# GNN layer end on one Trainium2 core: Wo and W2 products from high and low parts, W1 chunk by chunk

## The chip, the cores and the metric

The kernel runs on one core of one Trainium2 chip. The metric is the device time of one execution in microseconds (us); of several runs the median counts.

## The reference, cut to what matters

Four graph network layers follow each other on 1250 nodes with 512 features, everything in float32. The second of them is a stack of two attention layers over 40000 edges; the change is in the end of each of these two:

```python
for l in range(L):                       # L = 2, H = 8, D = 512, F = 256
    q = ((x @ Wq[l].T + bq[l]) * scaling).reshape(n, H, DH)
    k = (x @ Wk[l].T).reshape(n, H, DH)
    v = (x @ Wv[l].T).reshape(n, H, DH)
    ...                                  # softmax over the edges of each target
    agg = jax.ops.segment_sum(w[:, :, None] * v[srcidx], tgt, num_segments=n)
    attn = agg.reshape(n, D) @ Wo[l].T + bo[l]
    x = _batchnorm(x + attn, g1[l], beta1[l])
    ff = jax.nn.relu(x @ W1[l].T + b1[l]) @ W2[l].T + b2[l]
    x = _batchnorm(x + ff, g2[l], beta2[l])
return _layernorm(x, ln_g, ln_b)
```

The batch norm is over the nodes, so each feature needs all 1250 nodes of its row before it can be normalised. The other three layers, which take most of the 2642 us, are not touched.

## The kernel before

Features lie on partitions. `k.x1t` holds x as 4 blocks (KC) of 128 features by NP = 1280 node columns; `at.agg` holds the attention's result in the same form. The columns go in three pieces of C3 = 417 (WIDE). For each of the two layers `layer1` calls `attend`, whose block ends with a barrier of all engines, and then `finish_layer`. Each engine has its own program there, written out by hand; semaphores join them, and each engine's instructions run in the order in which the code has them.

TensorE in `finish_layer`: `turn(0, KC)` transposes Wo (four sets of four 128x128 transposes, into banks 0 and 1 in turn), and ScalarE copies each set to `wo` (L1581). `product(wo, at.agg, ...)` makes 12 outputs (4 feature blocks, three pieces each), each a sum over 4 input chunks, in a ring of four banks (2 to 5), as whole float32 matmuls (L1556). After 4 of them come the transposes of W1 and W2 (OTHERS). The product with W1 makes 6 outputs of 4 chunks, the hidden layer `hid`, by ScalarE's Relu (L1598); its first output waits chunk by chunk for the normalised x (`x_ready`), and after two outputs (WEIGHTS) the 16 transposes of the next layer's Wq come in between. The product with W2 makes 12 outputs of 2 chunks. Then, in layer 0 alone, `project_tensor` begins with the next layer's q, k and v. These already work with high and low parts: a high part is the value rounded to the type float32r (`F32R`), the low part is the rest, and three matmuls (high x high, high x low, low x high) stand for one float32 product (L1142).

VectorE in `add_and_norm`: for each output it adds bias and x from the bank (L1643, which frees the bank); after three outputs it takes the statistics of that feature block (L102, L104, L108), ScalarE takes the root (L1585), and one block later VectorE makes scale and shift (L1624 to L1626) and normalises (L1631). In the second norm of layer 0 ScalarE writes the high part and the whole x (L1608, L1611) and VectorE the low part (L1636). Between the two norms it makes the low parts of the next Wq (L1133; ScalarE's high parts: L1126).

GpSimd, in layer 1 alone, adds a row to ten blocks (L1530) once all of x is normalised the first time. SyncE loads W1, W2 and Wq at the block's start, Wk after the last output of Wo, and Wv when Wq's transposes are done.

## Time and profile before

| | us |
|---|---|
| median of three runs | 2642.36 (2640.85 to 2644.28) |
| the profiled execution | 2644.61 |
| its span, first to last instruction | 2642.9 |
| TensorE matmuls busy | 2421.8 (92%) |
| VectorE busy | 2058.8 (78%) |
| ScalarE busy | 1713.2 (65%) |
| GpSimd busy | 1090.7 (41%) |

The span is cut by the page into 40 slices of 66 us; a digit is the busy share in tenths. Layer 0's end runs from 1111 us and layer 1's from 1591 us of the span, and both are small parts of it, so they are read from the trace, by timeline. There a row is a start, a duration, the engine, the line of the kernel, the operation with output and inputs, how often it comes in a row, and in brackets how long the engine had been idle and what released it. A whole float32 matmul stands in the trace as two records, and the records of matmuls overlap a little: the pace is the distance between starts, not the duration of one. A stretch of windows gives for each engine the busy time and the number of instructions, then TensorE's granted clock as a share of 2.4 GHz.

### The profile page before, as it was taken

The numbers are of one execution on the slowest core, as the hardware profiler recorded it, in microseconds if no ns is written. First come the engines' busy times: TensorE is split into PE (matmuls) and PEld (weight loads), VectorE is DVE, ScalarE is ACT, GpSimd is POOL, SyncE is SP. The second block draws the span as 40 slices with busy tenths as digits, with TensorE's granted clock in tenths as the row PEclk, the third lists the DMA queues.
The fourth block names the chain that finished last, engine by engine and source line by source line (L and its number), as shares of the span: only waits on it lengthen the run. The fifth ranks groups of instructions, "written<-read, shape, count | busy, mean of one in ns | idle before, by whom it ended". The sixth has DMA issues, their size and how long they took to land. (4 is left out here: it accounts for less than half of the span.)

```text
span 2642.9 us, 44424 instructions
## 1 busy us (share of the span) xinstructions
PE 2421.8 (92%) x12731; PEld 1923.7 (73%) x12731; DVE 2058.8 (78%) x4101; ACT 1713.2 (65%) x3755; POOL 1090.7 (41%) x1061
## 2 busy tenths in 40 slices
PE   6999699998998999999999998798999999986887
PEld 3777455556798999858799994366777777765776
DVE  8789799998636888645588983756999999865757
ACT  1889788885726777614477871233999999835560
POOL 1776655524203454000254421115777777700311
PEclk9999899999999999999999999898999999988999
DMA  2004122213254434103444521124777777812101
GB/s 93 3 3 125 32 69 66 65 36 100 88 185 108 117 101 109 53 32 135 112 121 117 110 45 64 48 76 142 244 238 238 238 237 238 203 53 68 48 9 40
DMA packets 116594, 278.11 MB, mean 105 GB/s; under 512 B 24039, under 2 KB 38314, under 8 KB 116462
## 3 DMA queue, kind: packets, MB, share of 16 engines
q0 software_dynamic: 51328, 138.78, 19.3%
q1 hardware_dynamic: 65134, 137.65, 16.7%
q8 instruction: 73, 1.20, 0.2%
q14 instruction: 59, 0.48, 0.1%
HBM read 208.80 MB, written 59.43 MB: 101 GB/s over the span
## 5 line engine op out<-in xcount | busy, mean ns | idle before, releaser
L806 POOL DMA_INDIRECT feature_rows<-in_edge_attr,id_idx x352 | 341.9, 971 | 448.6 <-POOLq L1507 226.6
L2081 POOL DMA_INDIRECT x_got<-table_dram,src_idx x352 | 376.0, 1068 | 110.0 <-issue 82.0
L1441 DVE TENSOR_TENSOR pt_low<-bank,pt_high 128x640 fp32r<-128x640 f32 x320 | 262.8, 822 | 53.8 <-ACT pt_high L1404 52.6
L761 ACT ACTIVATE hot_rest<-hot_dst,slot_w 128x128 bf16<-128x128 bf16 x864 | 272.9, 399 | 43.9 <-DVE hot_dst L711 43.5
L1404 ACT CAST pt_high<-bank 128x640 fp32r<-128x640 f32 x320 | 220.3, 689 | 113.5 <-PE bank L1355 113.5
L2225 DVE TENSOR_TENSOR msg<-bank,x_got 128x512 f32<-128x512 f32 x352 | 236.6, 683 | 43.8 <-DMA x_got<-table_dram,src_idx 19.3
L1435 DVE CUSTOM_DVE_ANT_0 p<-bank,log_counts 128x1254 f32<-128x1254 f32 x160 | 232.8, 1455 | 14.1 <-PE bank L1338 14.1
L1355 PE MATMUL bank<-ident,p 128*128 128x128 f32 x1600 | 229.3, 275 | 2.4 <-DVE pt_low L1441 2.4
L1396 ACT ACTIVATE p<-p,bound 128x1254 f32<-128x1254 f32 x160 | 215.5, 1347 | 9.3 <-DVE bound L1435 9.3
L1366 PE MATMUL bank<-pt_high,val 128*128 128x256 f32 x800 | 212.7, 300 | 0.9 <-DVE agg_t L1447 0.9
L2205 DVE SCALAR_TENSOR_TENSOR msg_low<-msg,msg_high 128x512 fp32r<-128x512 f32 x308 | 209.3, 680 | 0.0
L2170 ACT ACTIVATE msg_high<-msg 128x512 fp32r<-128x512 f32 x308 | 193.5, 628 | 18.5 <-DVE msg L2225 17.8
L1367 PE MATMUL bank<-pt_low,val 128*128 128x256 f32 x800 | 199.7, 284 | 0.0
L1355 PEld LDWEIGHTS bank<-ident,p 128*128 128x128 f32 x1600 | 190.7, 142 | 11.4 <-issue 3.2
L217 POOL DMA_INDIRECT slots_dram<-rec,pos x152 | 152.2, 1002 | 112.9 <-issue 95.1
L1337 PE MATMUL bank<-keys,queries 128*128 128x418 f32 x480 | 186.2, 388 | 12.8 <-DVE bound L1435 7.5
L1338 PE MATMUL bank<-keys,queries_low 128*128 128x418 f32 x480 | 172.2, 359 | 0.0
L782 PE MATMUL bank<-hot_src,hot_rest 128*128 128x417 bf16 x864 | 170.8, 339 | 0.0
L809 POOL DMA_DIRECT2D features_dram<-feature_rows x88 | 51.2, 582 | 274.6 <-DMA feature_rows<-in_edge_attr,id_idx 274.6
L582 PE MATMUL bank<-row_hot,col_part 125*128 125x352 f32 x840 | 156.6, 339 | 8.6 <-ACT col_part L625 4.5
L582 PEld LDWEIGHTS bank<-row_hot,col_part 125*128 125x128 f32 x840 | 135.4, 190 | 29.5 <-issue 18.6
L1367 PEld LDWEIGHTS bank<-pt_low,val 128*128 128x128 f32 x800 | 154.2, 193 | 0.0
(435 smaller groups left out, 6347.4 us busy)
## 6 DMA issues: line engine op xcount, KB each, us to landing
features_dram<-feature_rows POOLq DMA_DIRECT2D x88, 256.0 KB
edge_got<-features_dram SPq DMA_DIRECT2D x88, 256.0 KB, 3.6
qk_dram<-qk_high SPq DMA_DIRECT2D x16, 640.0 KB, 2.9
qk_dram<-qk_low SPq DMA_DIRECT2D x16, 640.0 KB, 4.2
keys<-qk_dram SPq DMA_DIRECT2D x32, 320.0 KB, 4.9
queries<-qk_dram SPq DMA_DIRECT2D x32, 320.0 KB, 6.9
queries_low<-qk_dram SPq DMA_DIRECT2D x32, 320.0 KB, 8.8
acc_a<-zeros SPq DMA_DIRECT2D x1, 6400.0 KB
```

The lines of the kernel that those rows point to most:

```text
L582: m = pe.matmul(ps_p[:, q, :], col_part[0:EP, u, q, :], row_hot[0:EP, u, :], start=(c == 0), stop=(c == PE_COLS - 1))
L761: last = act.activation(hot_rest[:, u, j, q, :], hot_dst[:, u, :, j], ACT.Copy, scale=k.slot_w[:, 1 + q, bass.ds(tile0 + j, 1)])
L806: pool.indirect_dma_start(out=self.rows[:, u, t % GT * ED:(t % GT + 1) * ED], out_offset=None, in_=self.a.edge_attr_128, in_offset=bass.In ...
L1355: t = pe.transpose(unit(i)[:, j * P:(j + 1) * P], p[:, n % AHEAD, (u * HALF + j) * P:(u * HALF + j + 1) * P], k.ident[:])
L1366: pe.matmul(to, v, p_high[:, slot, j, :], start=(u == 0 and j == 0), stop=False)
L1367: x = pe.matmul(to, v, p_low[:, slot, j, :], start=False, stop=(u == 1 and j == HALF - 1))
L1396: act.activation(rows, rows, ACT.Exp, bias=bound[:, n % 4:n % 4 + 1], scale=-1.0, accum_out=sums[:, n // (2 * NB) % 2, n % NB, n // NB % 2 ...
L1404: act.copy(p_high[:, made % 3, :, n % 2 * P:(n % 2 + 1) * P], unit(2 * n + u).rearrange("p (j n) -> p j n", n=P)).then_inc(high_made, 1)
L1435: dve.tensor_tensor_reduce(out=thirds(p[:, n % AHEAD, :]), in0=k.bank[:, 0:3, 0:THIRD], in1=thirds(k.log_counts[:, n % NB, :]), scale=-1.0 ...
L1441: dve.tensor_tensor(p_low[:, made % 3, :, columns], unit(2 * n + u).rearrange("p (j n) -> p j n", n=P), p_high[:, made % 3, :, columns].bi ...
L2081: pool.indirect_dma_start(out=xg[:, g % XRING, j, :], out_offset=None, in_=k.table_dram, in_offset=bass.IndirectOffsetOnAxis(ap=k.src_idx[ ...
L2225: dve.tensor_tensor(msg[:, j, :], k.bank[:, 2 + j, :], xg[:, r, j, :], ALU.add).then_inc(added_x, 1)
```

## The change

The function `finish_layer` is changed, and nothing else.

- Wo and the aggregate are split. ScalarE writes the aggregate's high part chunk by chunk (four casts of 128x1280), each ahead of the copy of a turned chunk of Wo, which is now that chunk's high part. VectorE makes the low part of each. They lie where the next layer's high and low x come later.
- The third and fourth set of Wo's transposes wait for the low part of the first and second (`w_lowered`).
- The first six outputs of Wo are made together, in a ring of six banks: for each input chunk three passes for each of six outputs. Then W1 and W2 are transposed, then come the other six outputs one by one.
- All ten copies of turned weights now stand ahead of ScalarE's first root. W2's two low parts are made by VectorE after the seventh add.
- W1 stays whole float32 but goes chunk by chunk over all six outputs. Two sets of the next Wq's transposes stand ahead of the last chunk, two behind W1.
- ScalarE makes the hidden layer twice, rounded and whole; VectorE makes its low part (L1717 in the changed file) before W2's adds. W2 takes three passes.
- The pieces are 418, 418 and 416 columns (EVEN) in place of 417.

```diff
+    FP = FF // P
+    agg_parts = [Region(nc, at.wq_at - 4 * KC * NP * (2 - q), at.wq_at - 4 * KC * NP * (1 - q)).take(f"agg_{n}", [P, KC, NP], F32R) for q, n in enumerate(("high", "low"))]
+    r = Region(nc, at.wo_rows_end, at.wq_at - 2 * 4 * KC * NP)
+    wo = r.take("wo_in", [P, 2, KC, D], F32R)
     w1 = r.take("w1_in", [P, KC, FF], F32)
-    w2 = r.take("w2_in", [P, FF // P, D], F32)
...
-    hid = r.take("hidden", [P, FF // P, NP], F32)
-    FP = FF // P
-
-    OTHERS = 4
-    WEIGHTS = 2
+    hid_whole = r.take("hidden_whole", [P, 2, C3 + 1], F32)
+
+    w2 = Region(nc, at.wo_rows_end - 4 * KC * D - 2048, at.wo_rows_end).take("w2_in", [P, 2, FP, D], F32R)
+
+    over_agg = Region(nc, at.agg_end - 4 * KC * NP, at.agg_end)
+    hid = over_agg.take("hidden", [P, 2, FP, NP], F32R)
+    RING = 6
+    EARLY = 2
+
     affine_ready = S("bn_affine_ready")
 
-    turns = [(0, c, KC, wo[:, c, :]) for c in range(KC)] + [(1, c, FP, w1[:, c, :]) for c in range(KC)] + [(2, c, KC, w2[:, c, :]) for c in range(FP)]
+    turns = [(0, c, KC, wo[:, 0, c, :]) for c in range(KC)] + [(1, c, FP, w1[:, c, :]) for c in range(KC)] + [(2, c, KC, w2[:, 0, c, :]) for c in range(FP)]
+    low_parts = [(n, wo[:, 1, n, :]) for n in range(KC)] + [(2 * KC + c, w2[:, 1, c, :]) for c in range(FP)]
...
@@ -1535,36 +1542,65 @@
                 for n, (j, c, o, to) in list(enumerate(turns))[first:end]:
                     if c == 0:
                         pe.wait_ge(w_loaded[j], 16)
-                    if n >= 2:
+                    if 2 <= n < 2 + KC:
+                        pe.wait_ge(w_lowered, n - 1)
+                    elif n >= 2:
                         pe.wait_ge(w_copied, n - 1)
                     turned(pe, k, n % 2, rows[j], c, o).then_inc(w_turned, 1)
 
...
+            def out_of(n, ring):
+                o, (c, wide) = n // 3, EVEN[n % 3]
+                return k.bank[:, 2 + n % ring, 0:wide], slice(o * P, (o + 1) * P), slice(c, c + wide)
+
+            def rows_of_wo(n, i):
+                to, o, c = out_of(n, RING)
+                for q, s in ((0, 0), (0, 1), (1, 0)):
+                    m = pe.matmul(to, wo[:, q, i, o], agg_parts[s][:, i, c], start=(i == 0 and q + s == 0), stop=(i == KC - 1 and q == 1))
+                return m
 
             turn(0, KC)
-            pe.wait_ge(w_copied, KC)
-            product(wo, at.agg, KC, KC, o_done, o_added, None, lambda: turn(KC, len(turns)), OTHERS)
+            for i in range(KC):
+                pe.wait_ge(w_lowered, i + 1)
+                pe.wait_ge(agg_low_made, i + 1)
+                for n in range(RING):
+                    m = rows_of_wo(n, i)
+                    if i == KC - 1:
+                        m.then_inc(o_done, 1)
+            turn(KC, len(turns))
+            for n in range(RING, 3 * KC):
+                pe.wait_ge(o_added, n - RING + 1)
+                for i in range(KC):
+                    m = rows_of_wo(n, i)
+                m.then_inc(o_done, 1)
             pe.wait_ge(w_copied, len(turns))
-            pe.wait_ge(o_added, 9)
-            product(w1, k.x1t, KC, FP, h_done, h_copied, x_ready, turn_following if following else None, WEIGHTS)
-            pe.wait_ge(h_copied, 3 * FP)
-            product(w2, hid, FP, KC, f_done, f_added)
+            for i in range(KC):
+                if i == KC - 1 and following:
+                    turn_following(0, EARLY)
+                pe.wait_ge(x_ready, i + 1)
+                for n in range(3 * FP):
+                    to, o, c = out_of(n, RING)
+                    if i == 0:
+                        pe.wait_ge(o_added, 3 * KC - RING + n + 1)
+                    m = pe.matmul(to, w1[:, i, o], k.x1t[:, i, c], start=(i == 0), stop=(i == KC - 1))
+                    if i == KC - 1:
+                        m.then_inc(h_done, 1)
+            if following:
+                turn_following(EARLY, KC)
+            pe.wait_ge(w_lowered, len(low_parts))
+            for n in range(3 * KC):
+                if n < 3:
+                    pe.wait_ge(h_low_made, 3 * (FP - 1) + n + 1)
+                if n >= 4:
+                    pe.wait_ge(f_added, n - 3)
+                to, o, c = out_of(n, 4)
+                for i in range(FP):
+                    for q, s in ((0, 0), (0, 1), (1, 0)):
+                        m = pe.matmul(to, w2[:, q, i, o], hid[:, s, i, c], start=(i == 0 and q + s == 0), stop=(i == FP - 1 and q == 1))
+                m.then_inc(f_done, 1)
 
...
@@ -1577,6 +1613,8 @@
         def _(act):
             def copies(first, end):
                 for n, (j, c, o, to) in list(enumerate(turns))[first:end]:
+                    if n < KC:
+                        act.copy(agg_parts[0][:, n, :], at.agg[:, n, :]).then_inc(agg_high_made, 1)
                     act.wait_ge(w_turned, n + 1)
                     act.copy(to, k.bank[:, n % 2, 0:o * P]).then_inc(w_copied, 1)
 
@@ -1584,19 +1622,22 @@
                 act.wait_ge(var_ready, turn * KC + o + 1)
                 act.sqrt(norm.dev[:, o:o + 1], norm.var[:, o:o + 1]).then_inc(dev_ready, 1)
 
-            copies(0, KC)
+            copies(0, len(turns))
             for o in range(KC):
                 root(0, o)
-                if o == 0:
-                    copies(KC, len(turns))
+            if following:
+                for c in range(EARLY):
+                    weight_high(act, k, following, 0, c)
             for n in range(3 * FP):
-                if following and n == WEIGHTS:
-                    for j in range(KC):
-                        weight_high(act, k, following, 0, j)
                 act.wait_ge(h_done, n + 1)
-                c = WIDE[n % 3]
-                act.activation(hid[:, n // 3, c:c + C3], k.bank[:, 2 + n % 4, 0:C3], ACT.Relu,
-                               bias=at.vec[:, at.B1 + n // 3:at.B1 + n // 3 + 1]).then_inc(h_copied, 1)
+                (c, wide), bias = EVEN[n % 3], at.vec[:, at.B1 + n // 3:at.B1 + n // 3 + 1]
+                act.activation(hid[:, 0, n // 3, c:c + wide], k.bank[:, 2 + n % RING, 0:wide], ACT.Relu, bias=bias)
+                if n >= 2:
+                    act.wait_ge(h_low_made, n - 1)
+                act.activation(hid_whole[:, n % 2, 0:wide], k.bank[:, 2 + n % RING, 0:wide], ACT.Relu, bias=bias).then_inc(h_copied, 1)
+            if following:
+                for c in range(EARLY, KC):
+                    weight_high(act, k, following, 0, c)
             if following:
                 act.copy(following.x_high[:, :, W3:NP], k.x1t[:, :, W3:NP])
             for o in range(KC):
@@ -1616,7 +1657,11 @@
         def _(dve):
             me = Steps(nc, dve, at.sem("finish_dve"))
 
-            def add_and_norm(done, added, bias, gain, beta, turn):
+            def low_part(n, to):
+                dve.wait_ge(w_copied, n + 1)
+                dve.tensor_tensor(to, k.bank[:, n % 2, :], turns[n][3].bitcast(F32), ALU.subtract).then_inc(w_lowered, 1)
+
+            def add_and_norm(done, added, bias, gain, beta, turn, ring):
 
                 def normalise(o):
                     dve.wait_ge(dev_ready, turn * KC + o + 1)
@@ -1637,15 +1682,19 @@
...
                 for n in range(3 * KC):
-                    o, c = n // 3, WIDE[n % 3]
-                    x = k.x1t[:, o, c:c + C3]
+                    o, (c, wide) = n // 3, EVEN[n % 3]
+                    end = min(c + wide, W3)
+                    x = k.x1t[:, o, c:end]
                     dve.wait_ge(done, n + 1)
-                    dve.scalar_tensor_tensor(x, k.bank[:, 2 + n % 4, 0:C3], at.vec[:, bias + o:bias + o + 1], x, ALU.add, ALU.add).then_inc(added, 1)
+                    dve.scalar_tensor_tensor(x, k.bank[:, 2 + n % ring, 0:end - c], at.vec[:, bias + o:bias + o + 1], x, ALU.add, ALU.add).then_inc(added, 1)
                     if n % 3 == 0 and o:
                         normalise(o - 1)
+                    if not turn and n == RING:
+                        for m, to in low_parts[KC:]:
+                            low_part(m, to)
                     if n % 3 == 2:
                         dve.wait_ge(added, n + 1)
-                        norm.stats(dve, me, o, *(k.x1t[:, o, c:min(c + C3, N)] for c in WIDE))
+                        norm.stats(dve, me, o, *(k.x1t[:, o, c:min(c + wide, N)] for c, wide in EVEN))
                         norm.variance(dve, me, var_ready, o, o + 1)
                         if turn and following and o:
                             lower(o - 1)
@@ -1653,12 +1702,23 @@
                 if turn and following:
                     lower(KC - 1)
 
-            add_and_norm(o_done, o_added, at.BO, at.G1, at.BETA1, 0)
+            for i in range(KC):
+                dve.wait_ge(agg_high_made, i + 1)
+                dve.tensor_tensor(agg_parts[1][:, i, :], at.agg[:, i, :], agg_parts[0][:, i, :].bitcast(F32), ALU.subtract).then_inc(agg_low_made, 1)
+                low_part(*low_parts[i])
+            add_and_norm(o_done, o_added, at.BO, at.G1, at.BETA1, 0, RING)
 
             if following:
-                for c in range(KC):
+                for c in range(EARLY):
                     weight_low(dve, k, following, 0, c)
-            add_and_norm(f_done, f_added, at.B2, at.G2, at.BETA2, 1)
+            for n in range(3 * FP):
+                c, wide = EVEN[n % 3]
+                dve.wait_ge(h_copied, n + 1)
+                dve.tensor_tensor(hid[:, 1, n // 3, c:c + wide], hid_whole[:, n % 2, 0:wide], hid[:, 0, n // 3, c:c + wide].bitcast(F32), ALU.subtract).then_inc(h_low_made, 1)
+            if following:
+                for c in range(EARLY, KC):
+                    weight_low(dve, k, following, 0, c)
+            add_and_norm(f_done, f_added, at.B2, at.G2, at.BETA2, 1, 4)
             if following:
                 project_vector(dve, me, k, following)
             else:
```

ScalarE's program at the start of layer 0's end. Before:

```order
L1581 COPY wo_in<-bank 128x512 x4
L1585 ACT_TABLE_LOAD
L1585 ACTIVATE bn_dev<-bn_var 128x1
L1581 COPY w_in<-bank 128x256 x4
L1581 COPY w_in<-bank 128x512 x2
```

And now, the same place (`bn_dev<-bn_var` is the root):

```order
L1617 CAST agg_high<-agg_t 128x1280
L1619 CAST wo_in<-bank 128x512
...
L1619 COPY w_in<-bank 128x256 x4
L1619 CAST w_in<-bank 128x512 x2
L1623 ACT_TABLE_LOAD
L1623 ACTIVATE bn_dev<-bn_var 128x1 x4
```

Casts of the aggregate have come in front of the copies (four pairs in all), and the table load has moved behind the copies of W1 and W2.

TensorE from the end of the Wo product in layer 0 to the start of W2. Before:

```order
L1556 MATMUL bank<-agg_t,wo_in 128x417 x32
L1556 MATMUL bank<-x1t,w_in 128x417 x8
L1055 MATMUL bank<-ident,wqkv_rows_a_7127 128x128 x16
L1556 MATMUL bank<-x1t,w_in 128x417 x16
L1556 MATMUL bank<-hidden,w_in 128x417 x24
```

And now, the end of the third round over W1's six outputs, and the fourth:

```order
L1588 MATMUL bank<-x1t,w_in 128x418 x2
L1588 MATMUL bank<-x1t,w_in 128x416
L1055 MATMUL bank<-ident,wqkv_rows_a_7127 128x128 x8
L1588 MATMUL bank<-x1t,w_in 128x418 x2
L1588 MATMUL bank<-x1t,w_in 128x416
L1588 MATMUL bank<-x1t,w_in 128x418 x2
L1588 MATMUL bank<-x1t,w_in 128x416
L1055 MATMUL bank<-ident,wqkv_rows_a_7127 128x128 x8
L1602 MATMUL bank<-hidden,w_in 128x418 x12
```

The transposes of Wq have been split, eight ahead of W1's last round and eight behind it.

VectorE from the end of the first norm to the second norm's first adds, in layer 0. Before:

```order
L1625 TENSOR_TENSOR bn_shift<-bn_mean_var,bn_scale 128x1
L1626 TENSOR_TENSOR bn_shift<-vec,bn_shift 128x1
L1631 TENSOR_SCALAR x1t<-x1t,bn_scale,bn_shift 128x1251
L1133 TENSOR_TENSOR wqkv_a_7132<-bank,wqkv_a_7132 128x512 x4
L1643 SCALAR_TENSOR_TENSOR x1t<-bank,vec,x1t 128x417 x3
```

And now:

```order
L1670 TENSOR_TENSOR bn_shift<-bn_mean_var,bn_scale 128x1
L1671 TENSOR_TENSOR bn_shift<-vec,bn_shift 128x1
L1676 TENSOR_SCALAR x1t<-x1t,bn_scale,bn_shift 128x1251
L1133 TENSOR_TENSOR wqkv_a_7132<-bank,wqkv_a_7132 128x512 x2
L1717 TENSOR_TENSOR hidden<-hidden_whole,hidden 128x418 x2
L1717 TENSOR_TENSOR hidden<-hidden_whole,hidden 128x416
L1717 TENSOR_TENSOR hidden<-hidden_whole,hidden 128x418 x2
L1717 TENSOR_TENSOR hidden<-hidden_whole,hidden 128x416
L1133 TENSOR_TENSOR wqkv_a_7132<-bank,wqkv_a_7132 128x512 x2
L1689 SCALAR_TENSOR_TENSOR x1t<-bank,vec,x1t 128x418 x2
```

Six subtractions for the hidden layer have come between the low parts of Wq and the adds.

## Rows read from the trace of the kernel before

**Rows 1.** The page, TensorE's granted clock in 40 slices (9: 0.9 or more):
```profile
PEclk9999899999999999999999999898999999988999
```

**Rows 2.** Windows (PE, PEld, DVE, ACT, POOL busy, PEclk), layer 0: Wo part, second norm:
```profile
1115.50:1152.00 36.50, 35.94 (x113) 19.98 (x114) 17.51 (x41) 4.26 (x10) 0.00 (x0) 1.00 0.08 30
...
1181.00:1199.00 18.00, 16.75 (x57) 10.19 (x56) 17.31 (x44) 9.19 (x9) 0.00 (x0) 1.00 0.00 0
```

**Rows 3.** Timeline of TensorE, layer 0:
```profile
1111.13 3.73 PE L1055 MATMUL bank<-ident,wo_rows 128*128 128x128 f32 x16 [1.92 <-PEq L1308]
1115.54 11.47 PE L1556 MATMUL bank<-agg_t,wo_in 128*128 128x417 f32 x32 [0.68 <-ACT wo_in L1581]
...
1129.58 22.57 PE L1556 MATMUL bank<-agg_t,wo_in 128*128 128x417 f32 x64
1151.98 2.26 PE L1556 MATMUL bank<-x1t,w_in 128*128 128x417 f32 x6
1156.94 3.77 PE L1556 MATMUL bank<-x1t,w_in 128*128 128x417 f32 x10 [2.70 <-DVE x1t L1631]
...
1163.70 11.37 PE L1556 MATMUL bank<-x1t,w_in 128*128 128x417 f32 x32
1175.77 17.07 PE L1556 MATMUL bank<-hidden,w_in 128*128 128x417 f32 x48 [0.70 <-ACT hidden L1598]
```

**Rows 4.** The same, layer 1:
```profile
1590.96 3.73 PE L1055 MATMUL bank<-ident,wo_rows 128*128 128x128 f32 x16 [1.92 <-PEq L1308]
1595.37 6.97 PE L1556 MATMUL bank<-agg_t,wo_in 128*128 128x417 f32 x13 [0.68 <-ACT wo_in L1581]
...
1633.97 2.26 PE L1556 MATMUL bank<-x1t,w_in 128*128 128x417 f32 x6
1638.94 14.97 PE L1556 MATMUL bank<-x1t,w_in 128*128 128x417 f32 x42 [2.71 <-DVE x1t L1631]
```

**Rows 5.** Timeline, the next layer's q: first and last of 13 low-part passes:
```profile
1196.73 0.35 PE L1142 MATMUL bank<-px_low,wqkv_a 128*128 128x418 f32 x1
...
1203.62 0.35 PE L1142 MATMUL bank<-px_low,wqkv_a 128*128 128x418 f32 x1
```

**Rows 6.** Groups of ScalarE: busy us, mean ns of one, idle before:
```profile
L1928 ACT CAST at<-at_raw 128x1280 fp32r<-128x1280 f32 x10 | 12.6, 1266 | 39.5 <-PE bank L1048 39.5
...
L1208 ACT COPY qk_whole<-bank 128x418 f32<-128x418 f32 x16 | 8.1, 509 | 28.0 <-PE bank L1142 28.0
...
L1598 ACT ACTIVATE hidden<-bank,vec 128x417 f32<-128x417 f32 x12 | 7.3, 610 | 27.5 <-PE bank L1556 27.5
...
L1581 ACT COPY wo_in<-bank 128x512 f32<-128x512 f32 x8 | 4.7, 586 | 14.7 <-PE bank L1055 14.7
```

**Rows 7.** Groups of VectorE, the same columns:
```profile
L1133 DVE TENSOR_TENSOR wqkv_a<-bank,wqkv_a 128x512 fp32r<-128x512 f32 x16 | 10.6, 686 | 12.5 <-ACT wqkv_a L1126 12.5
...
L1636 DVE TENSOR_TENSOR px_low<-x1t,px_high 128x1280 fp32r<-128x1280 f32 x3 | 4.4, 1482 | 0.0
...
L1636 DVE TENSOR_TENSOR px_low<-x1t,px_high 128x418 fp32r<-128x418 f32 x2 | 1.2, 595 | 2.4 <-ACT x1t L1611 2.4
```

**Rows 8.** Timeline of VectorE, second norm: layer 0, and layer 1's first statistics:
```profile
1180.96 1.58 DVE L102 BATCH_NORM_STATS2 bn_pieces<-x1t 128x6 f32<-128x417 f32 x3
...
1205.44 0.62 DVE L1636 TENSOR_TENSOR px_low<-x1t,px_high 128x444 fp32r<-128x444 f32 x1 [0.80 <-ACT x1t L1611]
...
1659.80 1.58 DVE L102 BATCH_NORM_STATS2 bn_pieces<-x1t 128x6 f32<-128x417 f32 x3
```

**Rows 9.** Windows (columns as in rows 2): start of layer 0's and layer 1's end:
```profile
1111.00:1115.50 4.50, 3.73 (x16) 3.00 (x16) 0.00 (x0) 2.35 (x4) 0.00 (x0) 0.55 0.73 233
...
1595.30:1599.80 4.50, 4.43 (x7) 2.28 (x8) 0.00 (x0) 1.30 (x2) 0.00 (x0) 0.51 0.83 304
```

**Rows 10.** Windows (columns as in rows 2), two other places, TensorE partly busy:
```profile
612.00:622.00 10.00, 6.63 (x51) 5.37 (x50) 7.22 (x2) 7.02 (x12) 3.66 (x4) 1.00 1.15 347
625.00:632.00 7.00, 3.41 (x13) 2.25 (x11) 6.93 (x3) 5.93 (x6) 7.00 (x3) 0.88 0.49 148
```

More of the change, by code:

```diff
@@ L1537, in turn, with turn_following @@
                         pe.wait_ge(w_loaded[j], 16)
-                    if n >= 2:
+                    if 2 <= n < 2 + KC:
+                        pe.wait_ge(w_lowered, n - 1)
+                    elif n >= 2:
                         pe.wait_ge(w_copied, n - 1)
                     turned(pe, k, n % 2, rows[j], c, o).then_inc(w_turned, 1)
-            def turn_following():
-                for c in range(KC):
+            def turn_following(first, end):
+                for c in range(first, end):
@@ L1544, in turn_following @@
                     turn_weight(pe, k, following, 0, c)
-            def product(w, x, inputs, outputs, done, free, arrive=None, others=None, at_n=None):
-                for n in range(3 * outputs):
-                    o, c = n // 3, WIDE[n % 3]
-                    if others and n == at_n:
-                        others()
-                    if n >= 4:
-                        pe.wait_ge(free, n - 3)
-                    for i in range(inputs):
-                        if arrive and n == 0:
-                            pe.wait_ge(arrive, i + 1)
-                        m = pe.matmul(k.bank[:, 2 + n % 4, 0:C3], w[:, i, o * P:(o + 1) * P], x[:, i, c:c + C3],
-                                      start=(i == 0), stop=(i == inputs - 1))
-                    m.then_inc(done, 1)
@@ L1654, in add_and_norm @@
                     lower(KC - 1)
-            add_and_norm(o_done, o_added, at.BO, at.G1, at.BETA1, 0)
+            for i in range(KC):
[3 more added lines that the diff above has]
+            add_and_norm(o_done, o_added, at.BO, at.G1, at.BETA1, 0, RING)
             if following:
-                for c in range(KC):
+                for c in range(EARLY):
                     weight_low(dve, k, following, 0, c)
-            add_and_norm(f_done, f_added, at.B2, at.G2, at.BETA2, 1)
+            for n in range(3 * FP):
[6 more added lines that the diff above has]
+            add_and_norm(f_done, f_added, at.B2, at.G2, at.BETA2, 1, 4)
             if following:
```

4 lines of the change are left out of this document (1 added, 3 removed).

## The prediction, on record before the changed kernel ran

> **What bounds the kernel now.** I read the page's forty slices first [rows 1]: the changed function is entered twice, for layer 0 near 1111 us and for layer 1 near 1591 us, some 90 us each, and TensorE's clock is near full there. Then the timeline of TensorE in each of the two [rows 3, 4]. The reader should see three parts. The Wo product runs without a gap, 96 records 0.35 us apart; a whole float32 product of 417 columns is two records, so 0.70 us. Then TensorE does three outputs' first chunks of W1 and waits 2.70 us for the normalised x. Then W1 and W2 run again at 0.70 us a product. Up to the end of W1 TensorE ends last: over the Wo part VectorE is busy 17.51 of 36.50 us [rows 2]. From there VectorE ends last: 17.31 of 18.00 us busy in the second norm [rows 2], which is 5.8 us for each of its blocks of 128 features, where TensorE needs 3 x 1.40 = 4.2. That chain begins with the statistics at 1180.96 and ends with the last low piece at 1206.06 [rows 8]. So what counts is how much earlier the second norm's VectorE chain may begin, in layer 0 and in layer 1 (1659.80 now). Cheaper W2 products are worth nothing behind that point.
>
> **The change, part by part.** All in span time of layer 0, then what differs in layer 1.
>
> (a) *The start, +2.2 us in each layer.* Four input chunks of Wo must now be split into high and low, and the aggregate too. ScalarE makes a high part of 128x1280 in 1.27 us [rows 6], then copies the turned weight in 0.59; VectorE follows with 1.48 for the aggregate's low part and 0.69 for the weight's [rows 7]. From 1111.1: high part 1112.4, low part 1113.9, weight low part 1114.6. The third set of transposes waits for that, the fourth for the second one, which is there 1.48 + 0.69 us later, at 1116.8. All four sets stand ahead of the first product in TensorE's queue. A set takes a quarter of 3.73 us [rows 3], so the first product starts at 1117.75, against 1115.54 now. Queued behind this wait is only the product; VectorE and ScalarE are ahead of it from then on, since a chunk takes TensorE 3.4 us and VectorE 2.2. The price can't be much below (VectorE's 4.3 us of work is in series); it could be 3.5 with slow handovers.
>
> (b) *The Wo product, -6.1 us in each.* 48 products become 144 passes. The projection's passes of the same 418 columns and type stand in the trace: 13 records of the low part from 1196.73 to 1203.62, 12 steps of three passes [rows 5], so 0.574 for three and 0.191 for one. 48 x 0.70 = 33.6 becomes 48 x 0.574 = 27.5. The transposes of W1 and W2 stay between (2.7 us), now after six outputs in place of four. The Trainium skill, page "TensorE: Matmul & The Clock Gate", section "Back-to-back issue gap", gives N/2.4 + 2.5 ns for a warm matmul, 0.177 us at 418 columns; the rows show 0.191, and they decide. By the page the product would take 25.4 us, the layers would gain 2 us more each, and the time would be about 2625 us.
>
> (c) *The clock, +2.2 us in layer 0, 0 in layer 1.* TensorE is at 1.2 GHz (granted clock 0.50 to 0.55) through the transposes in both layers, after some microseconds with little work [rows 9]. In layer 0 it was at full clock from the first product, in layer 1 only 4.4 us after it: 13 records took 6.97 us [rows 4]. The change spreads the transposes out and so gives TensorE less to do ahead of the first product. I take layer 1's case for both: 4.4 us at half clock lose 2.2, which layer 1 has already. Bounds: 0 in both (2.2 better in layer 1, 2.2 better in layer 0), or much longer, which is a rival below.
>
> (d) *W1, chunk by chunk.* Its 24 products stay whole float32, 16.8 us. What goes is the wait of 2.70 for the last norm [rows 3]: the last chunk is needed only 12.6 us after the product's start. VectorE has to be done by then. Its first add comes late (when six outputs are almost complete, about 1130.7), and ScalarE's table load of 1.28 us now stands behind ten copies, so the first root comes at about 1137.8 and VectorE stands for 2.5 us. From there it needs about 5.8 us a block, plus 1.4 for W2's two low parts, against 6.9 of TensorE for three outputs: its last normalised block comes near 1157.6, and TensorE asks for it near 1163. So the wait is gone, with 5 us of cover. W1's first round waits for the banks of the last adds; at most 0.5. In layer 0 eight of the next layer's transposes stay inside W1 (1.0 us), the other eight go behind it, where TensorE would wait for the hidden parts.
>
> W1 now starts at 1151.98 and ends at 1175.07 [rows 3]. After: start at 1151.98 + 2.2 - 6.1 + 2.2 = 1150.3, end at + 16.8 + 1.0 = 1168.1, **7.0 earlier**. Layer 1: 1633.97 + 2.2 - 6.1 = 1630.1, end at 1646.9, against 1638.94 + 14.97 = 1653.91 [rows 4]: **7.0 earlier**.
>
> (e) *The hidden's low parts, +0.9 in layer 0, about 0 in layer 1.* The six outputs of W1 are now completed 0.70 apart in the last round, the first 3.5 us before W1's end. For each ScalarE does two activations; alone one takes 0.61, in a row 0.51 [rows 6]. I take 1.1 for a pair, 6.6 in all, so 3.1 past W1's end; with VectorE's subtraction of 0.60 [rows 7] 3.8. W2's first output needs the fourth low part, 1.6 past the end, and is done at +2.8; the third, needing the sixth, at +5.0; its add ends at +5.8. Today the statistics behind the third add begin at 1180.96, 5.9 after W1's end [rows 8]. In layer 0 two high and two low parts of the next Wq stand ahead of the adds on VectorE (at most 2 x 0.69, partly waiting for ScalarE): adds from +4.9, the third done at +6.8, so 0.9 later. With ScalarE at 1.22 a pair it is 0.7 more in each. In layer 1 GpSimd's ten additions, which wait for the last normalised x, now partly run beside VectorE's subtractions; no row shows this pair together, I take 0 and keep 0.5 for the range.
>
> (f) *W2, 0.* 72 passes, 1.15 us an output, three in 3.4, while VectorE needs 5.8 a block. All of it lies beside VectorE. The loads of K's and V's weights move by -2 and +5 us, and are used tens of microseconds later.
>
> **Sum.** Layer 0: 7.0 - 0.9 = 6.1. Layer 1: 7.0. Together 13.1 us. The profiled execution took 2644.61 us (span 2642.90) and would take 2631.5; the median of the three runs, 2642.36, is 2.25 us below that execution, so the forecast is **2629.3 us**. What comes behind each layer's end waits for its barrier and moves as a whole: GpSimd's gathers beside the attention don't end last.
>
> **Rivals.**
> *The clock doesn't fall back on us, or less* (first products at 2.4 GHz in both layers, as in layer 0 now): 4.4 us more, 17.5 in all, 2624.9. For it: layer 0 now. Against: fewer transposes in a row before the product.
> *The clock falls in W2.* TensorE would be busy 3.4 of 5.8 us there, 59%. At 66% the clock stayed 1.00, at 49% it came to 0.88 [rows 10]; 59% is between. At 1.2 GHz an output takes 2.3 us and three 6.9, more than VectorE's 5.8, so TensorE would be the bound, by 1.1 us a block in layer 0 and 1.5 in layer 1, until its full load brings the clock back. Some 4 us in all: gain 9, 2633.3.
> *The splitting chains are slower than their rows.* 1.5 us more at each start and 2.5 more at each hidden chain, from handovers that the prices above don't hold: 8 us, gain 5, 2637.3, within 0.2%.
> *The clock stays at half through the first six outputs, and the kernel is slower.* Their 72 passes take 13.75 us at full clock and 27.5 at half, so 11.6 more than I count in each layer: 23.2 - 13.1 = 10.1 us slower, 2652.5. It decides once half clock lasts over 17 us of products in each layer (4.4 counted, plus twice 6.55). Against it: 4.4 us in layer 1 [rows 4, 9], and TensorE has no gap after the first product.
> That three passes are no cheaper than a whole product is excluded by rows 5.
>
> **How the numbers follow.** Forecast 0.58; clock better 0.12; clock falling in W2 0.17; slower chains 0.09; clock stuck 0.04. The 8 in 10 range takes in the first three with their bounds (a: 1.3 us a layer, e: 0.7 a layer): 2624.0 to 2636.0. A difference under 0.2%, 5.3 us, is about what can't be told from none. Faster by more: 0.88; within: 0.08; slower: 0.04.
>
> **What would show it.** Right: the first product 6 to 7 us after the first transpose; passes 0.19 us apart; no wait of TensorE for the norm inside W1; W1's end about 57 us after the first transpose in layer 0 and 56 in layer 1 (63.9 and 62.95 now); VectorE busy over 90% from the third add to the layer's end, and the statistics of the second norm near 1175 and 1653 less what layer 0 gained. Wrong: TensorE waiting for x in W1, a granted clock below 1 after the first 5 us of products or in W2, or more than 6 us from W1's end to the second norm's first statistics in layer 1.

## The result, and the profile after

Four runs of the changed kernel have a median of 2630.02 us (2627.87 to 2632.13), four of the kernel before 2643.32 (2640.85 to 2648.54). The ratio is 0.9947, with a 95% interval from 0.9931 to 0.9963: 13.3 us shorter, faster by more than 0.2%. The forecast was 2629.3 within 2624.0 to 2636.0. The profiled execution's span is 2630.4 us, 12.5 less than before.

The whole moved as forecast, but not in the way that it was forecast. To compare the two layers' ends I measure from the first of Wo's transposes in each. From there to the first statistics of the second norm, behind which VectorE is the bound, it took 69.83 us in layer 0 and 68.84 in layer 1 [rows 3, 4, 8]. Now it takes 62.74 and 65.42: 7.1 and 3.4 us less, where 6.1 and 7.0 were forecast.

TensorE in layer 0, timeline (start, duration, engine, line, operation, count, idle time before and its releaser), against [rows 3]:

```profile
1112.82 1.94 PE L1055 MATMUL bank<-ident,wo_rows 128*128 128x128 f32 x8 [1.92 <-PEq L1308]
1116.23 1.11 PE L1055 MATMUL bank<-ident,wo_rows 128*128 128x128 f32 x4 [1.47 <-DVE wo_in L1662]
1118.23 1.12 PE L1055 MATMUL bank<-ident,wo_rows 128*128 128x128 f32 x4 [0.88 <-DVE wo_in L1662]
1119.00 0.70 PE L1562 MATMUL bank<-agg_high,wo_in 128*128 128x418 f32 x1
...
1151.21 13.10 PE L1588 MATMUL bank<-x1t,w_in 128*128 128x418 f32 x36
1164.14 1.04 PE L1055 MATMUL bank<-ident,wqkv_rows_a 128*128 128x128 f32 x8
1165.02 4.37 PE L1588 MATMUL bank<-x1t,w_in 128*128 128x418 f32 x12
1169.23 1.04 PE L1055 MATMUL bank<-ident,wqkv_rows_a 128*128 128x128 f32 x8
1170.80 11.59 PE L1602 MATMUL bank<-hidden,w_in 128*128 128x418 f32 x60 [0.53 <-DVE hidden L1717]
```

The two waits of the later transposes for VectorE's low parts are there, 1.47 and 0.88 us. The first product comes 6.18 us after the first transpose. W1 starts at 38.4 us and runs without a wait to 56.6; the 2.70 us before the last norm's chunk are gone.

Layer 1, the same engine, its first transposes and from W1 on, against [rows 4]:

```profile
1584.95 1.94 PE L1055 MATMUL bank<-ident,wo_rows 128*128 128x128 f32 x8 [1.92 <-PEq L1308]
...
1622.84 17.31 PE L1588 MATMUL bank<-x1t,w_in 128*128 128x418 f32 x48
1643.29 14.44 PE L1602 MATMUL bank<-hidden,w_in 128*128 128x418 f32 x60 [3.14 <-DVE hidden L1717]
```

W1 ends at 55.2 us, as in layer 0, but then TensorE stands for 3.14 us for the hidden layer's low parts. What VectorE and GpSimd do in that time, timeline:

```profile
1629.48 0.93 DVE L1676 TENSOR_SCALAR x1t<-x1t,bn_scale,bn_shift 128x1251 f32<-128x1251 f32 x1
1637.82 0.59 DVE L1717 TENSOR_TENSOR hidden<-hidden_whole,hidden 128x418 fp32r<-128x418 f32 x1 [7.41 <-ACT hidden_whole L1637]
1638.82 6.40 DVE L1717 TENSOR_TENSOR hidden<-hidden_whole,hidden 128x418 fp32r<-128x418 f32 x5 [0.40 <-ACT hidden_whole L1637]
1645.75 0.65 DVE L1689 SCALAR_TENSOR_TENSOR x1t<-bank,vec,x1t 128x418 f32<-128x418 f32 x1 [0.53 <-PE bank L1602]
1647.84 0.65 DVE L1689 SCALAR_TENSOR_TENSOR x1t<-bank,vec,x1t 128x418 f32<-128x418 f32 x1 [1.43 <-PE bank L1602]
...
1630.56 13.71 POOL L1537 TENSOR_TENSOR x_rows<-x_rows,ln_b_row 128x512 f32<-128x512 f32 x10 [76.92 <-DVE x1t L1676]
```

The last five subtractions take 6.40 us, back to back, where in layer 0 each took 0.59 at a pace of 1.00. All but the last of them lie beside GpSimd's ten additions, which end at 1644.27. Then the adds come 2.1 and 1.8 us apart. TensorE's granted clock tells why, in windows of the same stretch (PE, PEld, DVE, ACT, POOL busy with counts, clock, DMA):

```profile
1640.20:1643.30 3.10, 0.01 (x1) 0.04 (x1) 3.10 (x3) 2.31 (x6) 3.10 (x3) 0.86 0.00 0
1643.30:1650.40 7.10, 7.10 (x23) 6.82 (x24) 3.91 (x6) 0.48 (x1) 0.97 (x1) 0.58 0.00 0
```

In the gap the clock fell, and W2's first outputs ran at 1.2 GHz (0.58 over the stretch). So two of the signs that the prediction named as "wrong" are there: more than 6 us from W1's end to the statistics in layer 1 (10.2), and a granted clock below 1 in W2.

The rest of the 12.5 us: layer 0's end began 1.7 us later than before, the attention between was 0.6 shorter, and the stages behind layer 1 together 3.1 shorter. The code of these stages is the same, and the four runs of before lie 7.7 us apart; I count this as scatter. Its sum, 2.0 us, is what made the forecast of the whole look better than its parts.

### The profile page after: what moved, and what is told of

The parts are those of the page before. It is cut to its first block and busy times, and to the rows that moved or that the text cites. A ratio compares the mean times of both kernels' runs of the same rounds, so it can differ in the third digit from the quotient of the medians.

```text
span 2630.4 us, 44774 instructions
## 1 busy us (share of the span) xinstructions
PE 2405.5 (91%) x12875; PEld 1955.3 (74%) x12875; DVE 2088.5 (79%) x4133; ACT 1726.7 (66%) x3775; POOL 1093.5 (42%) x1061
```

## Experiments

All kernels below ran where the kernel before took 2838.5 to 2838.9 us in place of 2643 (2811.5 for four of them: the changed kernel's third execution, the two kernels under "The order alone, and Wo alone", and the second execution of W2 whole with spread transposes), and where whole times of one kernel scatter over 11 to 24 us. The layers' ends are hardly touched by that, so the experiments are read by their local times, each from one traced execution. The kernel before has a trace from the first setting only. Two more executions of the changed kernel show how far local times repeat.

> The changed kernel itself, beside the combinations on one chip. Both theories: first product 6.2 us after the first transpose, W1's end at 55 to 57 us in both layers. Theory A (GpSimd's additions slow VectorE's subtractions in layer 1): the five subtractions together take 6.4 us there again, and the second norm's first statistics come 7.9 us after W1's end if the clock stays, 10.2 if it falls; in layer 0 6.2. Rival B (it was one execution's accident): subtractions of 0.59 us in layer 1.

> The changed kernel once more, as the measure for the combination beside it. Both theories: its own local times again, statistics at 62.7 and 65.4 us; the whole 0.994 to 0.996 of the kernel before.

Statistics came at 62.84 and 65.53 in the first, at 61.83 and 62.90 in the second. W1 began between 37.5 and 38.5 us in layer 0 and between 37.7 and 38.0 in layer 1: after the first product the half clock lasted 4.3 us in layer 0 of the first trace and 2.6 in that of the third execution. The five subtractions took 6.40 and 6.41 us in layer 1. In the second the clock stayed up after the gap: 7.9 us from W1's end to the statistics in layer 1, not 10.2. So the slow subtractions come each time and cost 2.1 us (7.9 against 5.8 where nothing disturbs them, below); the clock's fall comes on top in some executions and costs 2.3. The ratios of the whole times to the kernel before were 0.996 (0.9938 to 0.9982) and 0.9945 (0.9926 to 0.9965).

**GpSimd out of the way.**

```diff
-            pool.wait_ge(x_ready, KC)
```

> GpSimd's ten additions no longer wait for the normalised x; all else as in the changed kernel. Theory A (VectorE's subtractions in layer 1 are slowed by GpSimd's additions beside them, and TensorE's clock falls in the gap that this makes): subtractions 0.59 us each, last one as in layer 0 within 2 us of W1's end, no gap of 3.1 us before W2, granted clock 1.00 in W2, statistics at about 60.5 us after layer 1's first transpose in place of 65.4; the additions now lie beside the first norm, which has some us of cover. Rival B (the gap is the clock's or the splitting chain's own doing): statistics stay at 65.

The six subtractions of layer 1 in this kernel (min/median/max ns), and then those of the changed kernel:

```profile
L1716 DVE TENSOR_TENSOR hidden<-hidden_whole,hidden x6: 591/594/595, 1757.5 to 1762.5; 128x418 fp32r<-128x418 f32 x4, 128x416 fp32r<-128x416 f32 x2
```

```profile
L1717 DVE TENSOR_TENSOR hidden<-hidden_whole,hidden x6: 574/1411/1660, 1637.8 to 1644.6; 128x418 fp32r<-128x418 f32 x4, 128x416 fp32r<-128x416 f32 x2
```

Only the time of GpSimd's work was changed, and the subtractions fell from a median of 1411 to 594 ns. W2 began 1.4 us after W1's end at a granted clock of 1.00, the statistics came 5.8 us after it, at 60.86 us in place of 65.42. The additions now ran beside the first norm's adds and statistics, and those kept their times:

```profile
1715.00 12.49 POOL L1536 TENSOR_TENSOR x_rows<-x_rows,ln_b_row 128x512 f32<-128x512 f32 x10 [68.39 <-DMA x_rows<-x_dram]
...
1723.51 1.80 DVE L1688 SCALAR_TENSOR_TENSOR x1t<-bank,vec,x1t 128x418 f32<-128x418 f32 x3 [9.37 <-PE bank L1561]
1725.34 1.58 DVE L102 BATCH_NORM_STATS2 bn_pieces<-x1t 128x6 f32<-128x418 f32 x3
```

So the cause of the slow subtractions is shown: VectorE's subtraction of two tiles in SBUF beside GpSimd's addition, not VectorE's work beside GpSimd as such. That the clock's fall comes from the gap which they make is only argued: behind a gap of 1.4 us it stayed up in two traces, behind one of 3.1 us it stayed up in two and fell in two. The Trainium skill says of the subtractions, on the page "SBUF — State Buffer", section "Who interferes with whom": a VectorE instruction with two SBUF inputs contends with a GpSimd instruction that reads SBUF, one with at most one SBUF input does not, outside the modes in which it uses two ports. The adds, with one input in a bank, and the statistics agree with it.

**W2 whole.**

```diff
-                    for q, s in ((0, 0), (0, 1), (1, 0)):
-                        m = pe.matmul(to, w2[:, q, i, o], hid[:, s, i, c], ...)
+                    m = pe.matmul(to, w2[:, i, o], hid[:, i, c], start=(i == 0), stop=(i == FP - 1))
...
-                if n >= 2:
-                    act.wait_ge(h_low_made, n - 1)
-                act.activation(hid_whole[:, n % 2, 0:wide], ...)
...
-                dve.tensor_tensor(hid[:, 1, n // 3, c:c + wide], hid_whole[:, n % 2, 0:wide], ...)
```

> W2 and the hidden layer go back to whole float32 (one activation an output, no subtraction, no low parts of W2); Wo's passes and W1's order stay as in the changed kernel. Theory A (W2's passes gain nothing behind VectorE, and their splitting costs): in layer 0 the second norm's first statistics stay within 1 us of 62.7 us after the first transpose; in layer 1, where the subtractions ran beside GpSimd, they come at 61 in place of 65.4, so the whole is some 4 us shorter than the changed kernel. Rival B (the passes carry part of the gain): statistics in both layers 2 us or more later than now, the whole longer.

Statistics at 61.92 and 60.22 us: 0.8 and 5.2 sooner than in the changed kernel's first execution, but 0.1 later and 2.7 sooner than in its third. Counted from W1's start the scatter of the start drops out: in layer 0 the statistics come 24.35 us after it in all three executions of the changed kernel and 23.67 here; in layer 1 23.10 with three passes and early additions, and 21.91 here. So W2's three passes gain nothing, and their splitting costs 0.7 us in layer 0 and 1.2 in layer 1, where GpSimd and the clock come on top. GpSimd's additions took 12.27 us here, as before the change (12.28), and 13.71 beside the subtractions.

**The start.**

```diff
-            turn(0, KC)
+            turn(0, 2)
             for i in range(KC):
...
+                if i + 2 < KC:
+                    turn(i + 2, i + 3)
```

> The third and fourth set of Wo's transposes go behind the first and second chunk of the product. Theory A (the start is paid by TensorE standing for the low parts of weights that it needs only later): first product 3.4 us after the first transpose in place of 6.2, W1's start and all behind it 2 to 2.5 us earlier in each layer. Rival B (the clock takes it back: more of the products fall in the half clock): W1's start less than 1 us earlier.

```profile
1695.69 1.94 PE L1055 MATMUL bank<-ident,wo_rows 128*128 128x128 f32 x8 [1.92 <-PEq L1308]
1699.10 0.72 PE L1562 MATMUL bank<-agg_high,wo_in 128*128 128x418 f32 x1 [1.47 <-DVE wo_in L1664]
```

The first product came at 3.41 us. W1 began at 36.5 us in both layers: 1.9 and 1.4 us sooner than in the changed kernel's first execution, 1.0 and 1.1 sooner than in its third. That is at or above the rival's 1 and below the 2 to 2.5 of theory A. Of the 2.8 us at the first product 0.7 are no gain: the two sets of transposes come later, between the chunks, 0.36 us each. The half clock lasted from the first product for 4.7 us here, against 4.3 and 3.5 in the changed kernel's first trace; at half the pace that takes back 0.2 and 0.6. This execution is also the second case in which the clock stayed up through the gap of layer 1:

```profile
1749.50:1752.60 3.10, 0.03 (x1) 0.00 (x0) 3.10 (x3) 2.31 (x6) 3.10 (x3) 1.00 0.00 0
1752.60:1757.40 4.80, 4.60 (x23) 4.24 (x24) 3.88 (x5) 0.57 (x1) 1.06 (x1) 1.00 0.00 0
```

The same gap, the same instructions, and a clock of 1.00 where it was 0.86 and 0.58: statistics 7.9 us after W1's end in layer 1.

**W1 output by output.**

```diff
-            for i in range(KC):
...
-                for n in range(3 * FP):
+            for n in range(3 * FP):
+                to, o, c = out_of(n, RING)
+                pe.wait_ge(o_added, 3 * KC - RING + n + 1)
+                for i in range(KC):
```

> W1 goes output by output again (the next Wq's first transposes in the wait of the first output), the rest as in the changed kernel. Theory A (chunk by chunk hides the wait for the last norm): a wait of 4 to 4.5 us inside W1's first output, W1's end 4 us later in both layers; statistics 3 us later in layer 0, but in layer 1 not later, since the hidden parts then come 2.8 us apart and mostly after GpSimd is done. Rival B: no wait, W1's end within 1 us.

```profile
1737.44 1.56 PE L1588 MATMUL bank<-x1t,w_in 128*128 128x418 f32 x4
1739.91 0.97 PE L1588 MATMUL bank<-x1t,w_in 128*128 128x418 f32 x2 [0.91 <-DVE x1t L1675]
1745.08 17.58 PE L1588 MATMUL bank<-x1t,w_in 128*128 128x418 f32 x42 [4.20 <-DVE x1t L1675]
```

In layer 1 the waits are 0.91 and 4.20 us (0.90 and 3.33 in layer 0). Behind them 42 records take 17.58 us, where they took 14.97 before [rows 4], so here too a part ran at half clock (granted 0.50 behind the wait). W1's end came 5.4 and 8.1 us later than in the changed kernel's first execution, not 4; the statistics 4.3 and 2.0 us later. I had expected layer 1 not to lose, and that was wrong by the clock's share and because the wait is longer with a Wo product that ends sooner.

**Wo whole, W2 as in the changed kernel.** Its high and low parts are left out; ring, chunks and the rest stay.

```diff
-                for q, s in ((0, 0), (0, 1), (1, 0)):
-                    m = pe.matmul(to, wo[:, q, i, o], agg_parts[s][:, i, c], ...)
+                return pe.matmul(to, wo[:, i, o], at.agg[:, i, c], start=(i == 0), stop=(i == KC - 1))
```

> Wo goes back to whole float32 products, in the same order (six outputs by chunk, then six one by one), with no high and low parts of the aggregate or of Wo; W1 and W2 as in the changed kernel. Forecast's terms: start at 4.4 us in place of 6.2, 48 products of 0.70 in place of 144 passes of 0.191, so W1's start 6.1 less 1.8 to 4.0 (with the clock) later than in the changed kernel, at 40.7 to 42.9 us, and W1's end at 58.6 to 60.8 in layer 0. If the passes' gain was eaten by their splitting and the clock, W1's start is no later than 38.4 us.

First product at 3.53 us (it no longer waits for all four sets), W1's start at 39.9 and 40.8, its end at 57.8 in both. Against the three executions of the changed kernel the three passes of Wo, with what they cost at the start, are worth 1.1 to 2.1 us in layer 0 and 2.5 to 2.8 in layer 1. The forecast had 1.7 and 3.9 by its own terms (6.1 less 2.2 for the start, and in layer 0 less 2.2 for the clock); the kernel with Wo whole starts 0.9 us sooner than the one before, which those terms didn't hold. Its statistics came at 63.97 and 65.80 us. In layer 1 the gap before W2 was only 2.15 us, since GpSimd's additions overlapped fewer subtractions, and the clock fell all the same:

```profile
1745.35:1747.50 2.15, 0.00 (x0) 0.03 (x1) 2.00 (x2) 1.75 (x5) 1.05 (x1) 0.99 0.00 0
1747.50:1751.00 3.50, 3.50 (x10) 3.35 (x11) 1.84 (x3) 0.99 (x2) 0.00 (x0) 0.52 0.00 0
```

**The order alone, and Wo alone.** Two kernels that combine these edits: the first with Wo, W2 and the hidden layer whole, the second with W2 whole and W1 output by output.

> Of the change only the order is kept (rings of six, Wo's first six outputs and W1 chunk by chunk, Wq's transposes split in two); Wo, W2 and the hidden layer are whole float32. Theory A (most of the gain is the order of W1, which hides the wait for the norm; the passes of Wo add little at this start, those of W2 nothing): W1's end at 57.8 us after the first transpose in both layers, first statistics of the second norm at 63.6 in layer 0 and 62.7 in layer 1, so 6 us a layer before the old kernel's 69.8 and 68.8, and better than the changed kernel in layer 1 (65.4). Rival B (the passes carry the gain): statistics at 67 or later.

> Of the change only Wo's three passes and its order are kept; W1 goes output by output, W2 and the hidden layer are whole float32. Theory A: the wait for the last norm comes back, 4 to 5 us long, and TensorE's clock may fall in it: W1's end at 61 to 63 us, statistics at 67 to 68 us in both layers, so 1 to 3 us a layer before the old kernel. Rival B (the passes carry the gain): statistics at 64 or sooner.

The order alone gave 64.65 and 62.66, Wo's passes with their order 67.79 and 66.28. The first is 5.2 and 6.2 us sooner than the kernel before, the second 2.0 and 2.6. Theory A's numbers hold within 1.1 us; the largest miss is W1's end with the order alone in layer 0, 58.9 for 57.8. The four stages tell where the gains lie (us; layer 0, layer 1):

| | first transpose to first product | to W1's start | W1 | W1's end to statistics |
|---|---|---|---|---|
| before | 4.41, 4.41 | 36.44, 38.60 | 23.09, 19.94 | 5.89, 5.89 |
| order alone | 3.53, 3.52 | 37.45, 37.22 | 17.87, 16.99 | 5.80, 4.93 |
| Wo's passes with their order | 6.19, 6.19 | 31.44, 32.13 | 24.37, 23.03 | 5.79, 4.93 |
| changed, first execution | 6.18, 6.18 | 32.21, 31.71 | 18.18, 17.30 | 6.17, 10.23 |

With the order alone the gain in W1 itself is 5.2 us in layer 0 and 3.0 in layer 1. In layer 0 the kernel before had a second wait inside W1, 1.03 us for Wq's low part, besides the one for the norm, and eight more transposes; layer 1 had only its wait of 2.71. The other 3.3 us of layer 1 are a start that waits chunk by chunk (0.9), a shorter stretch at half clock behind the first product (in the 1.4 us of the second stage), and a W2 that no longer waits for the whole hidden layer (1.0). In layer 0 the second stage is 1.0 longer, with about 2 us at half clock where the kernel before had none. Wo's passes save 5.0 and 6.5 us in their own stage, and pay 1.8 for the start and 1.3 and 3.1 in W1, where the waits for the norm came out longer (3.30 and 4.17 us) and the clock fell to 0.50 behind them.

**What can be better.** The combination of W2 whole with the spread transposes, and that of three passes everywhere with the spread transposes and the early additions:

> Two edits together: W2 and the hidden layer whole float32, and the third and fourth set of Wo's transposes behind the first two chunks. If the two gains of the single runs add up: first product at 3.4 us, W1's end at 54.3 in layer 0 and 53.5 in layer 1, first statistics of the second norm at 60.1 and 59 us, against 62.7 and 65.4 in the changed kernel; whole 5 to 9 us shorter than the changed kernel, and about 20 us shorter than the kernel before. If the start's gain is taken back by the clock, statistics at 61.9 and 60.2 as with W2 whole alone.

> Three passes for W2 kept; Wo's transposes spread as above and GpSimd's additions not waiting for x. If W2's passes are worth something once nothing disturbs their splitting: statistics at 59.7 in layer 0 and 59 in layer 1, no later than with W2 whole and the same start. If they are worth nothing: 0.8 us later in layer 0 and 0.6 in layer 1 than that kernel.

> W2 whole and Wo's transposes spread, once more, beside the changed kernel. By its traces' local times it should be 10 us shorter than the changed kernel (2.8 in layer 0, 7.5 in layer 1); if the rest of the kernel takes something of that back, under 5 us.

| statistics, us after the first transpose | layer 0 | layer 1 |
|---|---|---|
| before | 69.83 | 68.84 |
| Wo's passes with their order | 67.79 | 66.28 |
| the order alone | 64.65 | 62.66 |
| changed, three executions | 62.74, 62.84, 61.83 | 65.42, 65.53, 62.90 |
| changed, W1 output by output | 66.99 | 67.46 |
| changed, Wo whole | 63.97 | 65.80 |
| changed, additions early | 61.59 | 60.86 |
| changed, W2 whole | 61.92 | 60.22 |
| changed, transposes spread | 60.88 | 61.75 |
| ... and additions early | 60.62 | 60.31 |
| ... and W2 whole in place of that, two executions | 59.97, 60.65 | 57.95, 57.92 |

W2 whole with the spread transposes is the shortest in layer 1 and, within the scatter, in layer 0. Against it W2's passes, undisturbed, come out at 0 to 0.7 us later in layer 0 and 2.4 in layer 1, of which 1.2 lies ahead of W1 already (its start at 37.2 in place of 36.0, with the clock) and 1.2 is the splitting; so they are worth nothing even then. In whole times this kernel is at 0.9941 (0.9918 to 0.9964) of before in its first comparison, beside 0.996 for the changed one, and at 0.9916 (0.9895 to 0.9937) in the second, beside 0.9945. In the second the medians are 2787.83 and 2795.76: 7.9 us apart, where the local times of these two executions say 6.2 (the 10 expected came from executions in which the changed kernel's clock had fallen). The intervals overlap, so that it beats the changed kernel rests on the traces and on the same sign in both comparisons. The other kernels' whole times were 0.9929 of before for W2 whole, 0.9933 for the early additions, 0.993 for the spread transposes and 0.9948 for these with early additions, each within 0.2 to 0.3% either way. They don't tell these kernels apart. Each kernel not named here ran once.

## Why the prediction was right, and where it wasn't

**(a) The start** was forecast at +2.2 us and came at +1.8: VectorE's pair takes 2.00 us, not 2.17, since one instruction begins before the last one's record ends.

**(b) Wo's passes** are right: three passes 0.57 us apart in the warm part. From the first product to W1's start it took 32.2 us in layer 0, where the forecast's terms give 36.4 - 6.1 + 2.2 = 32.5.

**(c) The clock** is right: half clock for 4.3 us from the first product in layer 0 and 3.5 in layer 1, 4.4 forecast (2.6 and 2.9 in the third execution). Windows of the start, layer 0 (columns as above), against [rows 9]:

```profile
1112.80:1119.00 6.20, 3.83 (x17) 3.04 (x17) 4.92 (x5) 6.16 (x7) 0.00 (x0) 0.50 0.80 263
1119.00:1123.30 4.30, 4.30 (x14) 4.13 (x13) 3.17 (x4) 0.71 (x2) 0.00 (x0) 0.50 0.30 113
1123.30:1151.20 27.90, 27.38 (x149) 26.44 (x149) 15.12 (x35) 4.05 (x9) 0.00 (x0) 0.99 0.00 1
```

**(d) W1** is right. With (a) to (c) its end came 7.4 us sooner in layer 0 and 7.8 in layer 1, 7.0 forecast in both. The first root comes after the copies and the table load, and VectorE stood 3.34 us for it (2.5 forecast); the last block of x was normalised 6.2 us before TensorE asked for it (5 forecast):

```profile
1138.43 1.28 ACT L1623 ACT_TABLE_LOAD   x1
1139.72 0.20 ACT L1623 ACTIVATE bn_dev<-bn_var 128x1 f32<-128x1 f32 x1
...
1139.95 0.17 DVE L111 RECIPROCAL bn_dev<-bn_dev 128x1 f32<-128x1 f32 x1 [3.34 <-ACT bn_dev L1623]
...
1157.85 0.93 DVE L1676 TENSOR_SCALAR x1t<-x1t,bn_scale,bn_shift 128x1251 f32<-128x1251 f32 x1
```

**(e) The hidden's low parts** are where the prediction failed. In layer 0 it was too careful: ScalarE made a pair in 0.98 to 1.00 us, not 1.1, and the statistics came 6.2 us after W1's end, not 6.8.

```profile
1165.92 0.61 ACT L1634 ACTIVATE hidden<-bank,vec 128x418 fp32r<-128x418 f32 x1
1166.43 0.60 ACT L1637 ACTIVATE hidden_whole<-bank,vec 128x418 f32<-128x418 f32 x1
1166.92 0.61 ACT L1634 ACTIVATE hidden<-bank,vec 128x418 fp32r<-128x418 f32 x1
```

In layer 1 the term was forecast at about 0, with the sentence "no row shows this pair together, I take 0 and keep 0.5 for the range". It was 4.4: 10.2 us from W1's end to the statistics in place of 5.8. Of that the subtractions beside GpSimd are 2.1 (shown by the kernel with early additions), and the clock's fall in the gap is 2.3 (four executions have the same gap; two kept the clock, at 7.9 us, and two did not, at 10.2). The clock's part is argued and not tested by itself. The prediction had seen that the two run together and took 0 for want of a row. But the trace of the kernel before has the pair, behind layer 1's end: six subtractions of 128x512 of the same kind, and beside four of them GpSimd's additions (timeline; the last line is the four alone, min/median/max ns).

```profile
1725.58 8.01 DVE L1997 TENSOR_TENSOR h_low<-h_scaled,h_high 128x512 fp32r<-128x512 f32 x6
1735.33 0.69 DVE L1997 TENSOR_TENSOR h_low<-h_scaled,h_high 128x512 fp32r<-128x512 f32 x1 [1.75 <-ACT h_high L1921]
...
1726.59 6.45 POOL L1857 TENSOR_TENSOR x<-z,l_b_row 128x512 f32<-128x512 f32 x4 [14.51 <-ACT z L1912]
...
L1997 DVE TENSOR_TENSOR h_low<-h_scaled,h_high x4: 1745/1756/1775, 1726.8 to 1731.8; 128x512 fp32r<-128x512 f32 x4
```

Alone one took 0.69 us, the four beside the additions 1.75 to 1.78 each. So this term could have been priced before any run.

**(f) W2** at 0 is right for layer 0. In layer 1 VectorE waited for TensorE at W2's first three outputs, as it does at full clock too (adds 1.1 us apart in the third execution), and the half clock stretched that to 2.1 and 1.8: a part of the rival "the clock falls in W2" came true, but it fell in the idle gap ahead of W2. In layer 0 the clock stayed 1.00 through W2. It was 0.95 over the second norm, since from 1191.9 us the next layer's first passes ran at half clock for 3 us, and VectorE still ended last: 17.31 us busy of 18.00, as before.

```profile
1175.60:1193.60 18.00, 14.28 (x67) 12.50 (x67) 17.31 (x44) 9.21 (x9) 0.00 (x0) 0.95 0.00 1
```

**The sum** was 13.1 and the two layers gave 10.5; the whole gave 13.3 by the medians. That it lies 0.7 us from the forecast is in part luck, since about 2 us of the profiled execution's 12.5 came from stages that the change doesn't touch. What stays open is why the clock fell in the gap of 3.1 us in two executions and not in two others, and fell in one of 2.15; no run here was made to tell that.

## What to carry to other kernels

Take a change apart by its order and its arithmetic: here a new order, which puts the only chunk that is late behind everything else, gave 5 to 6 us a layer (5.2 and 3.0 of it in W1 itself). Passes at four fifths of the price gave 1 to 3, and nothing where another engine ends last. Before giving an engine new work, look at what else runs at that time, not only at whether the engine is idle: a subtraction priced at 0.59 us from an undisturbed row took up to 1.66 beside GpSimd. If no row near the change shows the pair, look for it in the rest of the trace: here it stood later in the same kernel. And where transposes wait for a step that only a later chunk needs, put them behind the earlier chunk's products.

## What the runs showed of the hardware

- VectorE's subtraction of two SBUF tiles (128x418) took 0.59 us alone and up to 1.66 beside GpSimd's addition of SBUF tiles (128x512: 0.69 and 1.75 to 1.78), which itself went from 12.3 to 13.7 us for ten. VectorE's adds with one input in a bank (0.65 a piece) and its statistics kept their time beside the same additions.
- The same idle gap of 3.1 us left the granted clock at 1.00 in two executions and brought it to 0.58 over the next 7 us in two others; that is worth 2.3 us here. With Wo whole it fell to 0.52 behind a gap of 2.15 us; behind the kernel before's wait of 2.70 and gaps of 1.4 it stayed 1.00. After a wait of 4.2 us in W1 42 records took 17.58 us in place of 14.97.
- A pair of activations of 128x418 from a bank takes ScalarE 0.98 us in a row, 0.49 each, though one's record says 0.61.
